# A Flamingo block on one core: attention unit and prologue in a new order, three banks for maximum scores, one for value products, two buffers for raw outputs, near-tile work in halves

## The chip, the cores and the metric

The kernel runs on one core of a Trainium2 chip. The metric is the device time of one execution in microseconds, taken as the median of several runs.

## What is computed

```python
x = x + tanh(g_xattn) * attention(ctx, ctx, layernorm(x), Wk, Wv, Wq, Wo, p_params)
x = x + tanh(g_ffn) * moe(layernorm(x), gate_w, bias, Wg, Wu, Wd, Wg_s, Wu_s, Wd_s)

# attention: B=4, 1024 queries, 154 keys, 16 heads of 16
scores = qh @ kh.T / 4 + rel          # rel: 9 learned values by clip(q - k, -4, 4)
scores = where(q >= k, scores, -1e30)
out = softmax(scores) @ vh @ Wo.T

# moe: 4096 tokens, 8 experts, 4 chosen by grouped top-k of sigmoid scores, and one shared
```

Since there are only 154 keys, the mask and the distance term vary only in the first two tiles of 128 queries of each batch; they are called the near tiles 0 and 1.

## The kernel before

Each engine has its own instruction list, written by hand; semaphores tie the lists together, and nothing reorders them.

**Prologue.** Inputs are loaded; the first half batch (512 queries) is normalised and turned (`transposes`), queries, keys and values are projected. High and low parts are kept (`x_hi`/`x_lo`, `q_out`/`q_lo`, `k_hi`/`k_lo`) so that fast matmuls keep precision. Then the maximum scores of the first half batch are made.

**Units.** The attention is eight units, `unit(b, h, ...)`, two per batch (h=0 and h=1, 512 queries each). The units of batches 1 and 2 are the body of a hardware loop, those of batches 0 and 3 are written out; the text calls the eight u0 to u7. A unit has 20 steps `i`. Each step makes one transposed score tile (`score`, into one of two PSUM banks `sT`), whose exponential ScalarE takes (`ex`); after five steps (a group `g`) the value products follow (`values`, into `oT`), which ScalarE copies to `raw` (`raw_out`). In between the unit does, for other units:

- the maximum scores of the next half batch (`max_scores`, L854, 32 tiles of 128 queries by two heads), each reduced on VectorE (`maximum`, L582). The two k of a pair use the two banks of `smax`, and one stands before the value product and one behind it. For near tiles ScalarE copies the scores out (`near`, L466) to `sx`; GpSimd builds their distance terms (`near`, L380, L392), VectorE adds them, takes the maximum and subtracts it (`tile0` L596 and L599, `tile1` L605 to L616), and GpSimd subtracts for tile 0 (L389);
- the negated maxima (`minus_max`), turned by TensorE (`max_T`, L866), copied to `mt` (`max_out`, L636) and spread by a DMA of SyncE (`m_stack`, L261) into the stack `qs`, for which the first score of the next unit waits;
- normalisation, turning and projection for the unit after the next; SyncE stacks its queries in two parts of six DMAs (`q_stack`, L250) and its keys (`k_stack`);
- the division of the unit before: SyncE takes the sums from `raw` through DRAM (`divisors`, L267 to L277), VectorE takes reciprocals and divides (`divide`, L648), TensorE projects (`project`, L930), VectorE adds the residual (L655).

Projections, turns and copies share two PSUM banks `work` in a fixed order of use (`X_USE` to `Y_USE`); each waits until the use before the last is read (`work_free`).

**Behind the units** the expert part loads its split weights, routes, and finishes the last division, projection and residual (`attend_divide`, `attend_finish`, `attend_residual`); 72 turns of gate, up and down products follow.

## Time and profile before

| | us |
|---|---|
| median of 3 runs | 740.97 (736.86 to 741.93) |
| the profiled execution | 738.62 |
| its span, first to last instruction | 736.7 |
| lead-in, to the first score of u0 | 65.1 |
| attention, u0 to u6 | 275.2 |
| u7 and the start of the expert part | 63.1 |
| the expert turns | 333.3 |
| mean granted TensorE clock | 0.929 of full |

A unit's length is read from the first score of one unit to the first score of the next. "Busy" is how long an engine had an instruction under way; the idle time in brackets at a row names what the instruction waited for last.

### The profile page before, as it was taken

The numbers are of one execution on the slowest core, as the hardware profiler recorded it, in microseconds if no ns is written. First come the engines' busy times: TensorE is split into PE (matmuls) and PEld (weight loads), VectorE is DVE, ScalarE is ACT, GpSimd is POOL, SyncE is SP. The second block draws the span as 40 slices with busy tenths as digits, with TensorE's granted clock in tenths as the row PEclk, the third lists the DMA queues.
The fourth block names the chain that finished last, engine by engine and source line by source line (L and its number), as shares of the span: only waits on it lengthen the run. The fifth ranks groups of instructions, "written<-read, shape, count | busy, mean of one in ns | idle before, by whom it ended". The sixth has DMA issues, their size and how long they took to land.

```text
span 736.7 us, 10646 instructions
## 1 busy us (share of the span) xinstructions
PE 628.5 (85%) x3384; PEld 484.8 (66%) x3384; DVE 460.5 (63%) x884; ACT 277.4 (38%) x501; POOL 176.7 (24%) x177
## 2 busy tenths in 40 slices
PE   3674968788878977888647999999999999999997
PEld 2553745457545754554325888888888888888886
DVE  3567657777578758762168475755747575665653
...
DMA packets 39856, 58.65 MB, mean 80 GB/s; under 512 B 7984, under 2 KB 21040, under 8 KB 39792
## 3 DMA queue, kind: packets, MB, share of 16 engines
...
HBM read 31.76 MB, written 4.85 MB: 50 GB/s over the span
## 4 chain that ended last, share of the span: by engine, by line
issue 49%; PE 20%; DVE 10%; POOL 8%; DMA 6%; SPq 3%; ACT 2%; POOLq 0%; DVEq 0%; ACTq 0%
POOL hl L1150 4%; PE oT L915 4%; PE smax L854 4%; SPq L277 2%; DMA qs<-mt 2%; DVE mx L582 2%; PE oT L919 2%; PE sT L895 2%; DMA at<-rden_d 2%; PE work L794 2%; PE sT L894 2%; DVE mx L609 1%; DMA rden_d<-dent 1%; POOL d L380 1%; PE work L825 1%
## 5 line engine op out<-in xcount | busy, mean ns | idle before, releaser
L1150 POOL TENSOR_TENSOR hl<-sg,hh 128x512 fp32r<-128x512 f32 x72 | 93.0, 1293 | 249.3 <-ACT hh L1193 249.3
L482 ACT ACTIVATE ex<-sT 128x512 f32<-128x512 f32 (+1 forms) x160 | 92.2, 590 | 152.1 <-PE sT L895 127.6
L1187 ACT ACTIVATE sg<-pg 128x512 f32<-128x512 f32 x72 | 43.0, 597 | 198.8 <-PE pu L1432 198.0
L854 PE MATMUL smax<-km,qs 96*128 96x308 f32 (+1 forms) x240 | 91.2, 412 | 27.1 <-DVE mx L582 19.3
L582 DVE TENSOR_REDUCE mx<-smax 128x2 f32<-128x308 f32 x184 | 82.9, 474 | 48.3 <-PE smax L854 45.4
L854 PEld LDWEIGHTS smax<-km,qs 96*128 96x128 f32 x240 | 47.8, 206 | 72.8 <-DVE mx L582 40.1
L1447 PE MATMUL py<-wxl,hh 128*128 128x256 f32 x288 | 81.8, 284 | 3.1 <-DVE x L1331 2.0
L1447 PE MATMUL py<-wxh,hl 128*128 128x256 f32 x288 | 80.9, 281 | 0.0
L1447 PE MATMUL py<-wxh,hh 128*128 128x256 f32 x288 | 80.6, 280 | 0.0
L1319 DVE TENSOR_TENSOR sg<-cwb,sg 128x512 f32<-128x512 f32 x64 | 67.2, 1050 | 11.3 <-DMA cwb<-cwt_d 8.4
L1314 DVE TENSOR_TENSOR sg<-pu,sg 128x512 f32<-128x512 f32 x72 | 49.2, 683 | 28.0 <-ACT sg L1187 26.6
L1432 PE MATMUL pg<-x2l,wxh 128*128 128x512 f32 x144 | 60.6, 421 | 4.1 <-issue 4.1
L895 PE MATMUL sT<-qs,ks 128*128 128x256 f32 (+1 forms) x128 | 52.9, 429 | 12.3 <-DMA qs<-mt 11.0
L1447 PEld LDWEIGHTS py<-wxl,hh 128*128 128x128 f32 x288 | 54.1, 188 | 9.0 <-DVE x L1331 4.3
L1432 PE MATMUL pg<-x2h,wxh 128*128 128x512 f32 x144 | 57.8, 401 | 0.0
L1432 PE MATMUL pu<-x2l,wxh 128*128 128x512 f32 x144 | 57.6, 400 | 0.0
L1432 PE MATMUL pg<-x2h,wxl 128*128 128x512 f32 x144 | 57.5, 400 | 0.0
L1432 PE MATMUL pu<-x2h,wxl 128*128 128x512 f32 x144 | 57.4, 399 | 0.0
L1432 PE MATMUL pu<-x2h,wxh 128*128 128x512 f32 x144 | 56.9, 395 | 0.0
L1447 PEld LDWEIGHTS py<-wxh,hl 128*128 128x128 f32 x288 | 54.1, 188 | 2.7
L1447 PEld LDWEIGHTS py<-wxh,hh 128*128 128x128 f32 x288 | 54.7, 190 | 0.0
L1193 ACT CAST hh<-sg 128x512 fp32r<-128x512 f32 x72 | 44.0, 612 | 9.6 <-DVE sg L1319 9.3
(152 smaller groups left out, 1124.1 us busy)
## 6 DMA issues: line engine op xcount, KB each, us to landing
...
```

The lines of the kernel that those rows point to most:

```text
L482: nc.scalar.activation(ex[:, g % 2, i % 5, q0:HALF], ST[i % 2][:, q0:HALF], ACT.Exp).then_inc(exp_s, 1)
L582: nc.vector.reduce_max(mx[:, m_tile(h, p), 2 * stk:2 * stk + 2], bank[:, k, 0:PAIR].rearrange("p (j k) -> p j k", j=2), AX_X).then_inc(mx_ ...
L854: last_one = nc.tensor.matmul(bank[:, k, 0:width], qs[0:96, s, tile * P:(tile + 1) * P], km[:, s, 0:width], start=True, stop=True)
L895: last_one = nc.tensor.matmul(out[:, q0:HALF], ks[:, s, j * KL:j * KL + P], qs[:, s, q], start=True, stop=True)
L915: nc.tensor.matmul(OT[g % 2][32 * j:32 * j + 32, :], va[:, 4 * g + j, :], ex[:, g % 2, j, :], start=True, stop=True)
L1150: nc.gpsimd.tensor_tensor(hl[:, i % R, :], sg[:, i % R, :], hh[:, i % R, :], ALU.subtract).then_inc(hl_done, 1)
L1187: nc.scalar.activation(sg[:, i % R, :], PG[i % RG][:], ACT.Silu).then_inc(sg_s, 1)
L1193: nc.scalar.copy(hh[:, i % R, :], sg[:, i % R, :]).then_inc(hh_s, 1)
L1314: done = nc.vector.tensor_tensor(sg[:, i % R, :], PU[i % RG][:], sg[:, i % R, :], ALU.mult)
L1319: nc.vector.tensor_tensor(sg[:, i % R, :], cwb[:, e % RC, :], sg[:, i % R, :], ALU.mult)\
L1432: last = nc.tensor.matmul(out_[:], wa[:, e, w], xa[:, u, c, :], start=first, stop=(c == C - 1 and wa is wxh and xa is xh))
L1447: last = nc.tensor.matmul(y, ha[:, i % R, q], wa[:, e, 2 * C * I:XW], start=(e == 0 and s == 0 and j % 2 == 0), stop=(e == NE1 - 1 and s = ...
```

## The change

- PSUM: `smax` has three single banks, used in turn by the tiles q = 2p + k (a ring); `oT` has one bank; in the prologue the ring has five banks (with `sT`).
- `ORDER` gives the maximum scores a new order, in which tile 2 stands between parts of tile 0; they begin at step 0, not 3, and both of a pair stand before the value product.
- In an h=0 unit keys are projected first (steps 1 to 4); turns move to steps 7 and 8, value inputs to 9 and 10, queries to 11 to 14; `minus_max` moves to step 16, `max_T` to 17, the two `project` to 16 and 18, `tile1` to 13 to 15 and 17, `k_hi` and `k_lo` to 16 to 18.
- `raw_first` and `raw` are used by turns, so `raw_out` waits for the division two units back; it moves to steps 4, 9, 14 and 19.
- `divide` goes from VectorE to GpSimd, in an h=1 unit between the distance terms and the subtraction of tile 0.
- Tile 0 and the reduction of tile 1 are done in halves of the heads.
- SyncE: the last `k_stack` and the context load move past `q_stack`; the second half of x is loaded before wv.
- Prologue: `selectors` come first on ScalarE, `k_hi` and `k_lo` go in the three parts of the key projection (`k_hi_first`, `k_lo_first`), the statistics of the second half batch and its normalisation come earlier, its queries are projected in four pieces at p = 6 to 9, and `tile0` at p = 11.
- `minus_max` makes its first part as -2x + x; the input of context has one more, empty batch.

```diff
+    raw_first = sb("raw_first", [P, NG, HALF])
+    raws = (raw_first, raw)
...
-    SM = ctx.enter_context(nc.psum_tensor("smax", [P, 2, HALF], F32))
+    SM = ctx.enter_context(nc.psum_tensor("smax", [P, 3, HALF], F32))
-    M_START = (SM, STP)
-    OT = [ctx.enter_context(nc.psum_tensor(f"oT{i}", [P, HALF], F32)) for i in range(2)]
+    MAX_BANKS = [SM[:, i, :] for i in range(3)]
+    M_START = MAX_BANKS + ST
+    OT = ctx.enter_context(nc.psum_tensor("oT", [P, HALF], F32))
...
-    X_USE, V_USE, Q_USE, K_USE, M_USE, Y_USE = (0, 11), 2, (3, 13), 5, (8, 15), (9, 16)
+    FIRST_USE, K_USE, X_USE, V_USE, Q_USE, Y_USE, M_USE = (0, 11), 0, (3, 11), 5, (6, 13), ((8, 10), (15, 17)), (9, 16)
     K_PARTS = (range(0, 3), range(3, 6), range(6, 8))
 
-    K_STEP, K_READ = (12, 13, 14, 14, 15, 15, 16, 16), (15, 16, 17)
-    M0, NM = 3, TU * NSTK // 2
-
-
-    DIVIDE, TILE0 = ((13, 14), (12, 13)), (10, 11)
+    K_READ = (3, 4, 5)
+    NM = TU * NSTK // 2
+    NEAR = NM
+    ORDER = ((0, 0), (0, 1), (2, 0), (2, 1), (0, 2), (0, 3), (1, 0), (1, 1),
+             (1, 2), (1, 3), (2, 2), (2, 3), (3, 0), (3, 1), (3, 2), (3, 3))
+    RING = 3
+    PER_MAX = 3 * NM
+
+    TILE0, TILE1 = (9, 10, 11, 12), (13, 14, 15)
...
-            if h == 0 and ahead:
-                sp.wait_ge(v_ps, b + 1)
-                sp.nop().then_inc(waited, 1)
-                sp.dma_start(ctxb[:], t["ctx"][b + 1]).then_inc(c_in, 16)
             if carry and (h == 0 or ahead):
                 sp.wait_ge(st_ps, NI * u)
                 q_stack(1 - h, 1)
+            if carry and h == 0:
+                k_stack(NG - 1)
+            if h == 1 and ahead:
+                sp.wait_ge(v_ps, b + 2)
+                sp.nop().then_inc(waited, 1)
+                sp.dma_start(ctxb[:], t["ctx"][b + 2]).then_inc(c_in, 16)
             if carry:
-                divisors(u - 1)
+                divisors(u - 1, 1 - h)
...
                 m_stack(b + 1, 0)
-                sp.wait_ge(st_ps, NI * (u + 1))
-                k_stack(NG - 1)
...
+        def divide(u, h):
+            pool.wait_ge(rden_in, 128 * (u + 1))
+            pool.wait_ge(shift_in, 64 * (u + 1))
+            pool.nop().then_inc(waited, 1)
+            for g in range(2):
+                nc.gpsimd.tensor_tensor(at[:, g, :], raws[h][:, g, :], at[:, g, :], ALU.mult).then_inc(at_s, 1)
...
+                for half in (slice(0, H // 2), slice(H // 2, H)) if i == 0 else (slice(0, H),):
...
+            if between is not None:
+                divide(between, 0)
+            for i, half in enumerate((slice(0, NSTK // 2), slice(NSTK // 2, NSTK))):
+                pool.wait_ge(sadd_s, 7 * b + 3 + i)
+                nc.gpsimd.tensor_tensor(keys[:, half], keys[:, half], largest[:, half], ALU.subtract).then_inc(sub0_s, 1)
...
+            if carry and not (h == 1 and ahead):
+                divide(u - 1, 1 - h)
             if h == 1 and ahead:
-                near(b + 1, False)
+                near(b + 1, False, u - 1)
                 pool.wait_ge(st_ps, NI * (u + 1))
...
-        def raw_out(u, g, start=False):
+        def raw_out(u, h, g):
             act.wait_ge(pv_ps, NG * u + g + 1)
-            if not start:
-                act.wait_ge(at_s, 2 * (u - 1) + g % 2 + 1)
-            nc.scalar.copy(raw[:, g, :], OT[g % 2][:]).then_inc(raw_s, 1)
+            if not (isinstance(u, int) and u < 2):
+                act.wait_ge(at_s, 2 * (u - 1))
+            nc.scalar.copy(raws[h][:, g, :], OT[:]).then_inc(raw_s, 1)
...
-                if i == 5 and carry:
-                    raw_out(u - 1, 3, start=(h == 1 and isinstance(b, int) and b == 0))
-                if i == 6 and ahead:
-                    x_hi(u + 2, NW0 + X_USE[h])
-                if i == 11 and ahead:
+                if i == 4 and carry:
+                    raw_out(u - 1, 1 - h, 3)
+                if i in (8, 9) and ahead:
+                    x_hi(u + 2, NW0 + X_USE[h], (i - 8,))
+                if i == 13 and ahead:
                     for part in range(2):
                         act.wait_ge(qs_in[1 - h][part], 16 * 6 * (b + h + 1))
-                if i in (11, 13) and ahead:
-                    q_out(u + 2, NW0 + Q_USE[h], ((i - 11) // 2,))
+                if i in (13, 15) and ahead:
+                    q_out(u + 2, NW0 + Q_USE[h], ((i - 13) // 2,))
                 if ahead and h == 1:
-                    if i == M0:
+                    if i == 0:
                         act.wait_ge(sub_s, 3 * (b + 1))
-                    if i >= M0 and i - M0 < NM and m_tile(0, i - M0) < 2:
-                        near(b + 1, i - M0)
-                if i in (14, 17, 19):
-                    raw_out(u, (14, 17, 19).index(i), start=not carry)
-                if ahead and h == 0 and i == 19:
-                    k_hi(b + 1, False)
-
+                    if i < NM and m_tile(0, i) < 2:
+                        near(b + 1, i)
+                if i in (9, 14, 19):
+                    raw_out(u, h, i // 5 - 1)
+                if ahead and h == 0 and i in (16, 17):
+                    k_hi(b + 1, (i - 16,))
...
+                if i < NM and (h == 0 or ahead and m_tile(mh, i) >= 2):
+                    maximum(mb, mh, i)
+                if i in (0, 1) and ahead:
+                    tile_stats(b + 1, h, (2 * i, 2 * i + 1))
+                if i == 2 and ahead:
                     norm_stats(b + 1, h)
-                if i in (3, 4) and ahead:
-                    normalised(b + 1, h, (2 * (i - 3), 2 * (i - 3) + 1))
-                if i == 6 and ahead:
-                    x_lo(u + 2, NW0 + X_USE[h])
+                if i in (5, 6) and ahead:
+                    normalised(b + 1, h, (2 * (i - 5), 2 * (i - 5) + 1))
                 if i in K_READ and ahead and h == 0:
                     part = K_READ.index(i)
                     k_in(b + 1, NW0 + K_USE + part, part)
-                if i == 10 and ahead and h == 0:
+                if i in (9, 10) and ahead:
+                    x_lo(u + 2, NW0 + X_USE[h], (i - 9,))
+                if i == 8 and carry:
+                    reciprocals(u - 1)
+                if i == 11 and ahead and h == 0:
                     v_in(b + 1, NW0 + V_USE, False)
-                if i == 9 and carry:
-                    reciprocals(u - 1)
-                if i in DIVIDE[h] and carry:
-                    divide(u - 1, (DIVIDE[h].index(i),))
                 if diagonal and i in TILE0:
                     tile0(b + 1, TILE0.index(i))
-                if i in (11, 13) and ahead:
-                    q_lo(u + 2, NW0 + Q_USE[h], ((i - 11) // 2,))
+                if i in (14, 16) and ahead:
+                    q_lo(u + 2, NW0 + Q_USE[h], ((i - 14) // 2,))
+                if diagonal and i in TILE1:
+                    tile1(b + 1, TILE1.index(i))
...
-                if i == 18:
+                if i == 16 and (h == 0 or ahead):
+                    minus_max(mb, mh)
+                if i in (16, 18):
+                    pr = (i - 16) // 2
+                    if carry:
+                        residual(b - 1 + h, 1 - h, pr, NW0 + Y_USE[h][pr])
+                    else:
+                        unused(1, b, Y_USE[h][pr])
+                if i == 17:
                     if h == 0 or ahead:
-                        minus_max(mb, mh)
-                        if diagonal:
-                            tile1(b + 1, 0)
                         max_out(mb, mh, NW0 + M_USE[h])
                     else:
                         unused(1, b, M_USE[h])
-                if i == 19:
                     if diagonal:
-                        tile1(b + 1, 1)
-                        tile1(b + 1, 2)
-                    if h == 0 and ahead:
-                        k_lo(b + 1)
-                    if carry:
-                        for pr in range(2):
-                            residual(b - 1 + h, 1 - h, pr, NW0 + Y_USE[h] + pr)
-                    else:
-                        unused(2, b, Y_USE[h])
+                        tile1(b + 1, 3)
+                if h == 0 and ahead and i in (17, 18):
+                    k_lo(b + 1, (i - 17,))
...
+        dve.wait_ge(x_in[0], 16)
+        tile_stats(0, 1)
+        norm_stats(0, 1)
         q_lo(0, 2)
-        dve.wait_ge(x_in[0], 16)
-        norm_stats(0, 1)
+        k_in(0, 4, 0)
+        k_in(0, 5, 1)
+        k_lo_first(0)
         normalised(0, 1)
-        for part in range(3):
-            k_in(0, 4 + part, part)
+        k_in(0, 6, 2)
         v_in(0, 7, True)
-        k_lo(0)
+        k_lo_first(1)
+        k_lo_first(2)
         x_lo(1, 8)
         for p in range(NM):
-            if p == NM // 2:
-                q_lo(1, 10)
             if m_tile(0, p) >= 2:
-                maximum(0, 0, p, M_START[p % 2])
-            if p == 8:
-                for part in range(2):
+                maximum(0, 0, p, M_START)
+            if p in (7, 9):
+                q_lo(1, 10, ((p - 7) // 2,))
+            if p == 11:
+                for part in range(4):
                     tile0(0, part)
         minus_max(0, 0, start=True)
...
+            q = 2 * p + k
+            if q == 0:
+                pe.wait_ge(mx_s, PER_MAX * b + NM * h)
+            elif q >= RING and is_near(h, q - RING):
+                pe.wait_ge(sx_s, NEAR * b + copied(q - RING + 1))
+            elif q >= RING:
+                pe.wait_ge(mx_s, PER_MAX * b + NM * h + reduced(h, q - RING + 1))
+            stack_scores(m_tile(h, p), p, k, MAX_BANKS[q % RING])
...
-                if not (start and g < 2):
-                    pe.wait_ge(raw_s, NG * u + g - 1)
+                if not (start and g == 0):
+                    pe.wait_ge(raw_s, NG * u + g)
                 for j in range(4):
-                    nc.tensor.matmul(OT[g % 2][32 * j:32 * j + 32, :], va[:, 4 * g + j, :], ex[:, g % 2, j, :],
+                    nc.tensor.matmul(OT[32 * j:32 * j + 32, :], va[:, 4 * g + j, :], ex[:, g % 2, j, :],
...
-                if seeks:
-                    max_scores(b + h, 1 - h, i - M0, 0)
+                if i < NM and (h == 0 or ahead):
+                    for k in range(2):
+                        max_scores(b + h, 1 - h, i, k)
                 if i in (1, 3) and carry:
                     values(b - 1 + h, 1 - h, NG - 1, i // 2)
                 if i > 5 and i % 5 in (1, 3):
                     values(b, h, i // 5 - 1, i % 5 // 2, start)
-                if seeks:
-                    max_scores(b + h, 1 - h, i - M0, 1)
-                if i in (5, 6) and ahead:
-                    transposes(u + 2, b, X_USE[h], (i - 5,))
-                if i in (7, 8) and ahead and h == 0:
-                    values_in(b + 1, b, V_USE, ((0, 1), (2, 3, 4))[i - 7])
-                if i in (9, 10, 11, 12) and ahead:
-                    queries(b, X_USE[h], Q_USE[h], (i - 9,))
-                if ahead and h == 0:
-                    keys(b + 1, b, K_USE, [s for s in range(NSTK) if K_STEP[s] == i])
-                if i == 19:
-                    if h == 0 or ahead:
-                        max_T(b + h, 1 - h, b, M_USE[h])
-                    if carry:
-                        for pr in range(2):
-                            project(b - 1 + h, 1 - h, pr, b, Y_USE[h] + pr)
+                if ahead and h == 0 and i in (1, 2, 3, 4):
+                    keys(b + 1, b, K_USE, (2 * i - 2, 2 * i - 1))
+                if i in (7, 8) and ahead:
+                    transposes(u + 2, b, X_USE[h], (i - 7,))
+                if i in (9, 10) and ahead and h == 0:
+                    values_in(b + 1, b, V_USE, ((0, 1), (2, 3, 4))[i - 9])
+                if i in (11, 12, 13, 14) and ahead:
+                    queries(b, X_USE[h], Q_USE[h], (i - 11,))
+                if i == 17 and (h == 0 or ahead):
+                    max_T(b + h, 1 - h, b, M_USE[h])
+                if i in (16, 18) and carry:
+                    pr = (i - 16) // 2
+                    project(b - 1 + h, 1 - h, pr, b, Y_USE[h][pr])
```

Rows of the change have its own line numbers.

TensorE at the end of the last h=0 unit, u6, before (`nm` are the negated maxima, `at` the divided outputs):

```order
L919 MATMUL oT<-ex,vb 128x384 [waits exp]
L854 MATMUL smax<-km,qs 128x308 [waits mx]
L899 MATMUL sT<-idr,tp 128x128 [waits exp]
L901 MATMUL sT<-qs,k 128x256 x2
L866 MATMUL work<-idr,nm 32x128 [waits nm,work_free]
L866 MATMUL work<-idr,nm 32x128 x3
L930 MATMUL work<-wo,at 128x256 [waits work_free,at]
L930 MATMUL work<-wo,at 128x256 x3
L930 MATMUL work<-wo,at 128x256 [waits work_free,at]
L930 MATMUL work<-wo,at 128x256 x3
L895 MATMUL sT<-qs,ks 128x512 [waits ms_in,exp]
```

The same place in the change:

```order
L998 MATMUL work<-wo,at 128x256 [waits work_free,at]
L998 MATMUL work<-wo,at 128x256 x3
L962 MATMUL sT<-idr,sx 128x128 [waits exp]
L962 MATMUL sT<-idr,sx 128x128
L963 MATMUL sT<-qs,ks 128x256
L933 MATMUL work<-idr,nm 32x128 [waits nm,work_free]
L933 MATMUL work<-idr,nm 32x128 x3
L962 MATMUL sT<-idr,sx 128x128 [waits exp]
L962 MATMUL sT<-idr,sx 128x128
L963 MATMUL sT<-qs,ks 128x256
L987 MATMUL oT<-ex,vb 128x384 [waits exp]
L998 MATMUL work<-wo,at 128x256 [waits work_free,at]
L998 MATMUL work<-wo,at 128x256 x3
```

The turn of the maxima (L866, now L933) has left its place behind the last score, and the two projections stand apart from each other and before scores that are still to come.

VectorE in the h=1 unit of the loop, before, from the work on tile 0:

```order
L599 TENSOR_REDUCE mx<-sx 128x16
L551 TENSOR_TENSOR ql<-work,qh 128x512
L645 REGISTER_ALU
L646 REGISTER_ALU
L648 TENSOR_TENSOR at<-raw,at 128x512 x2
L551 TENSOR_TENSOR ql<-work,qh 128x512
L581 REGISTER_ALU
L582 TENSOR_REDUCE mx<-smax 128x2
L581 REGISTER_ALU
L582 TENSOR_REDUCE mx<-smax 128x2
```

The same list in the change, around the second low part of the queries:

```order
L606 TENSOR_TENSOR ql<-work,qh 128x512
L681 REGISTER_ALU
L682 TENSOR_REDUCE mx<-sx 128x8
L648 REGISTER_ALU
L649 TENSOR_REDUCE mx<-smax 128x2
L648 REGISTER_ALU
L649 TENSOR_REDUCE mx<-smax 128x2
L682 TENSOR_REDUCE mx<-sx 128x8
L606 TENSOR_TENSOR ql<-work,qh 128x512
L696 ISA
L699 SCALAR_TENSOR_TENSOR nm<-mx 128x2x16
L702 SCALAR_TENSOR_TENSOR nm<-mx,nm 128x2x16
```

The second `ql`, which frees SyncE's first part of `q_stack`, stood ahead of eight reductions of `smax`; now it stands behind all of them and behind both halves of tile 1's maximum, and the division is gone.

GpSimd in the h=1 unit of the loop, before, with tile 0 subtracted (L389) ahead of tile 1's terms:

```order
L380 TENSOR_TENSOR d<-relr,cst 128x2048
L386 REGISTER_ALU
L389 TENSOR_TENSOR sx<-sx,mx 128x8x2x128
L362 REGISTER_ALU
L366 REGISTER_ALU
L369 COPY relc<-sx 128x64
```

The same list in the change, from tile 1's terms on:

```order
L417 TENSOR_TENSOR d<-relr,cst 128x512
L422 REGISTER_ALU
L423 TENSOR_TENSOR d<-d,cst 128x512
L370 ISA
L371 REGISTER_ALU
L374 TENSOR_TENSOR at<-raw_first,at 128x512 x2
L430 REGISTER_ALU
L431 TENSOR_TENSOR sx<-sx,mx 128x4x2x128
L430 REGISTER_ALU
L431 TENSOR_TENSOR sx<-sx,mx 128x4x2x128
```

The subtraction of tile 0 is now two instructions at the end, behind the division.

## Rows read from the trace of the kernel before

**Rows 1.** Windows: length, busy PE, PEld, DVE, ACT, POOL, granted clock, DMA share, GB/s.
```profile
0.00:65.10 65.10, 33.50 (x134) 26.17 (x135) 35.99 (x76) 18.72 (x37) 19.42 (x28) 0.75 0.59 165
...
103.20:145.10 41.90, 34.14 (x142) 19.84 (x142) 26.75 (x41) 20.57 (x44) 15.21 (x16) 0.87 0.38 89
145.10:185.50 40.40, 34.94 (x224) 25.49 (x224) 31.31 (x66) 17.56 (x30) 2.25 (x4) 1.00 0.34 78
185.50:225.10 39.60, 31.76 (x143) 18.85 (x143) 27.68 (x45) 20.46 (x44) 15.21 (x16) 0.91 0.39 95
225.10:306.00 80.90, 68.81 (x367) 45.76 (x367) 59.66 (x110) 38.13 (x74) 17.56 (x20) 0.94 0.36 85
306.00:340.30 34.30, 28.68 (x152) 19.38 (x153) 21.09 (x43) 13.13 (x24) 0.98 (x2) 0.90 0.57 167
340.30:403.40 63.10, 39.77 (x154) 23.62 (x155) 27.71 (x66) 25.31 (x42) 3.49 (x5) 0.81 0.17 45
403.40:736.70 333.30, 326.09 (x1872) 281.99 (x1872) 202.58 (x381) 106.19 (x177) 101.33 (x84) 0.99 0.19 61
```

**Rows 2.** Timeline of PE in u2 and u3.
```profile
179.53 0.61 PE L866 MATMUL work<-idr,nm 128*32 128x128 f32 x4 [0.96 <-DVE nm L627]
...
179.98 3.62 PE L930 MATMUL work<-wo,at 128*128 128x256 f32 x16
...
185.50 0.73 PE L895 MATMUL sT<-qs,ks 128*128 128x512 f32 x2 [1.91 <-DMA qs<-mt]
...
212.31 0.62 PE L854 MATMUL smax<-km,qs 96*128 96x308 f32 x1 [3.89 <-DVE mx L582]
...
225.09 0.43 PE L894 MATMUL sT<-idr,sx 128*128 128x128 f32 x2 [1.99 <-DVE tp L616]
```

**Rows 3.** Chain that ended last, in order of time, at the end of u2.
```profile
180.99 4.47 DMA qs<-mt
```

**Rows 4.** Timeline of SyncE's queue in u2 and u3.
```profile
170.83 1.31 SPq L250 DMA_DIRECT2D qs<-qh  x2
...
173.47 1.24 SPq L250 DMA_DIRECT2D qs<-qh  x2
...
180.99 0.59 SPq L261 DMA_DIRECT2D qs<-mt  x1
...
220.27 0.58 SPq L261 DMA_DIRECT2D qs<-mt  x1
```

**Rows 5.** Timeline of DVE in u3.
```profile
207.64 3.62 DVE L648 TENSOR_TENSOR at<-raw,at 128x512 f32<-128x512 f32 x2 [0.66 <-DMA at<-rden_d]
...
211.19 0.68 DVE L551 TENSOR_TENSOR ql<-work,qh 128x512 fp32r<-128x512 f32 x1
...
211.79 0.85 DVE L582 TENSOR_REDUCE mx<-smax 128x2 f32<-128x308 f32 x2
...
220.48 2.72 DVE L609 TENSOR_REDUCE mx<-sx 128x16 f32<-128x2464 f32 x1 [0.23 <-DVE mt L636]
```

**Rows 6.** GpSimd: timeline in u3.
```profile
206.47 3.61 POOL L389 TENSOR_TENSOR sx<-sx,mx 128x2048 f32<-128x2048 f32 x1 [4.72 <-DVE mx L599]
```

**Rows 7.** The page's costliest groups, GpSimd's first.
```profile
L1150 POOL TENSOR_TENSOR hl<-sg,hh 128x512 fp32r<-128x512 f32 x72 | 93.0, 1293 | 249.3 <-ACT hh L1193 249.3
```

**Rows 8.** Timeline of the prologue: PE.
```profile
34.19 0.39 PE L854 MATMUL smax<-km,qs 96*128 96x316 f32 x1 [1.92 <-DVE km L575]
...
65.11 0.66 PE L894 MATMUL sT<-idr,sx 128*128 128x128 f32 x2 [8.55 <-DVE tp L616]
```

**Rows 9.** Timeline of the prologue: GpSimd, then DVE.
```profile
41.04 3.65 POOL L380 TENSOR_TENSOR d<-relr,cst 128x2048 f32<-128x2048 f32 x1
...
59.68 0.66 DVE L605 TENSOR_TENSOR sx<-sx,d 128x480 f32<-128x480 f32 x1 [2.67 <-POOL d L392]
```

**Rows 10.** Timeline of SyncE in u6, of ScalarE in u7.
```profile
324.51 4.61 SPq L1107 DMA_DIRECT2D wx<-in_wx  x9
...
358.67 0.59 ACT L472 COPY raw<-oT 128x512 f32<-128x512 f32 x1 [5.86 <-DVE at L648]
```

260 lines of the change are left out of this document (138 added, 122 removed).

## The prediction

> **What bounds the kernel now.** I first cut the span at the first score of each unit [rows 1]. The expert turns take 333.3 us with TensorE busy for 326.1 of them; no line of them changes, so they stay. What the change can touch is the lead-in of 65.1 us, the units u0 to u6, and the 63.1 us of u7 with the start of the expert part. In the loop a batch costs 80.0 us (u2 40.4, u3 39.6) and the next 80.9. There TensorE is busy for 34.9 and 31.8 us and VectorE for 31.3 and 27.7: neither is full, the two wait for each other.
>
> Next the waits of TensorE in u2 and u3 [rows 2]. At the end of u2 it waits 0.96 us for the negated maxima, turns them, projects for 3.62 us and then waits 1.91 us for the spread of the maxima, whose DMA takes 4.47 us from issue to landing [rows 3]. In u3 it waits 3.89 us for a reduction and at the end 1.99 us for the subtractions of tile 1. The 3.89 us come from VectorE's queue [rows 5]: two divisions that stand there as 3.62 us together, during which GpSimd subtracts tile 0 for 3.61 us [rows 6]. Last the lead-in: the first maximum score starts at 34.2 us, and the first score waits 8.55 us [rows 8], because tile 1's terms come from GpSimd late, after a term of 3.65 us for tile 0 and the subtraction behind it [rows 9].
>
> **The lead-in.** The selectors fill a time in which ScalarE waits, the second half's statistics one in which VectorE waits, and the low parts of the keys are made in three parts while TensorE still projects. Walking VectorE's list with the old durations, the last low part is ready near 28.5 instead of 34.2: 5.7 us. Tile 0's scores are copied some 6 us earlier, so the two halves of its term (3.65 us together [rows 9]) end near 38.5, and tile 1's terms near 43, before VectorE asks. VectorE then is the chain: the last queries' low part near 39 to 40.5, two pairs of maxima, tile 0 in four parts of 1.15, four pairs at 0.85 [rows 5], `minus_max`, turn and copy 1.6, and then for tile 1 the add of 0.66 [rows 9], the reduction of 2.72 [rows 5] and 1.8 of subtractions. That gives 55 to 57.5; I take 56.1, a gain of 9.0. The 2.67 us wait for GpSimd [rows 9] is gone; what is late next is VectorE itself. Bounds: 7 (queries at half clock as before) and 11.5 (full clock).
>
> **An h=0 unit (u2, u4).** TensorE's instructions stay: of its 34.9 busy us [rows 1] some 31.4 are left when the rows at half clock are counted at full. The unit now ends by a different chain: second low part of the queries (step 16), six DMAs of `q_stack`, the DMA of the maxima, landing. SyncE's queue is what is new here. Before, the six were issued from 170.83 to 174.71, long before the maxima's at 180.99 [rows 4]; now they start only at step 16, and the maxima's stand behind them. TensorE's list up to step 15 is 15 scores (5.2), 15 pairs of maximum scores (4.4), three sets of value products (4.2), keys (4.4), turns (0.9), value inputs (1.8), queries (2.8): 23.7 us. I add 2 us for the half clock after the wait at the start, 2.5 us where turns and value inputs wait for VectorE (it must do pairs of maxima, keys and the normalisation first), 0.6 for changes between kinds of matmul: 28.8. Score, exponential, copy and low part bring 31.0; plus 3.9 for the six issues [rows 4], plus 4.5 for the DMA [rows 3], 39.4 against 40.4. The wait for maxima of 0.96 is gone, but the wait for the DMA grows from 1.91 to about 3, since only 3.6 us of work stand behind the turn. Bounds: 37.4 without the half clock and the changes, 41 if the DMA is held up by the six before it.
>
> **An h=1 unit (u3, u5).** The division leaves VectorE: 3.62 us of its queue [rows 5]. Pairs of maxima no longer stop TensorE for 3.89 us, since the ring lets it run three tiles ahead. But the start is paced by ScalarE, which copies 16 near tiles between its exponentials and frees the ring: its list ends step 8 near 13.5 us. From there VectorE has, up to the second low part, both `x_lo`, six pairs of maxima (6 x 0.8), tile 0 in four parts (4.6), tile 1's add and maximum (0.84 + 2.72), two low parts: 15.7 us with no gap. GpSimd works at the same time: half a term, tile 1's terms, the division, both subtractions. The price of that is in the trace: two divisions that with nothing on GpSimd take 1.3 us took 3.62, and the first began 1.2 us after GpSimd's 3.61 [rows 5, 6]. So a two-input instruction waits nearly to the end of GpSimd's. Three of VectorE's meet one now (two tile 0 adds, tile 1's add); I take 2.6 us for them, between 0 and 4. That puts the second low part at 13.5 + 15.7 + 2.6 = 31.8, where it stood at 211.87 - 185.50 = 26.4 before [rows 2, 5]. Then 3.9 us of issues [rows 4] and about 3.7 for the smaller DMA of the maxima: 39.3, against 39.6 and, for u5, 40.4. In u3 what ended last was tile 1 (1.99 us); now the subtractions of tile 1 (3 us) hide behind the DMA, and the DMA is last. Bounds: 36.5 with no meeting, 41 with all.
>
> The loop's two batches so come to 78.7 each: 80.0 - 78.7 = 1.3 and 80.9 - 78.7 = 2.2, together 3.5.
>
> The Trainium skill, SBUF — State Buffer, "Who interferes with whom", says that a VectorE instruction with two SBUF inputs contends with a GpSimd instruction that reads SBUF, the loser blocking fully, and that `tensor_reduce` never does. The 3.62 us beside 3.61 us [rows 5, 6] agree with the first; the second is why halves of the maxima would go unharmed. The rule speaks against putting the division on GpSimd in an h=1 unit.
>
> **The others.** u0 and u1 take 80.0 us together, from 65.1 to 145.1 [rows 1]. u0 has no old division and gets the same chain at its end: 0.5 gained. u1 was 41.9 [rows 1] because of a half clock after a long wait; as an h=1 unit it comes to 39.4: 2.5. Together 3.0.
>
> u6 has no projections for later batches and no near tiles. Its 34.3 us hold a wait for the division. Now the division goes: old outputs copied one step earlier, sums and reciprocals through DRAM as before (at 18 instead of 19 us), 2 x 1.29 on GpSimd [rows 7] = 20.6; projection, score and turn 23.2, copy 24; the DMA would land at 28.5. But the nine weight loads are issued from 324.51 to 329.1 [rows 10], 1 us earlier now, and their data fill the queues until about 29; the maxima's DMA stands behind them: 30.3. Gain 4.0, between 2 and 6.
>
> u7: ScalarE's wait of 5.86 for the division [rows 10] goes with the second buffer. TensorE instead waits at step 16 for the same division, which ends at 20 us of the unit (17.1 + 2.6), but only scores of three steps are left behind it where before six were: about 1.0 gained. In the start of the expert part the two divisions leave VectorE between routing and weights: 1.1. Together 2.1; bounds 0 and 4.
>
> One value bank, the raw buffers' extra SBUF, the six additional VectorE and GpSimd halves outside those counted: nothing, as the copy of `oT` stands two steps ahead of the next group's products.
>
> **The sum.** 9.0 + 3.0 + 3.5 + 4.0 + 2.1 = 21.6. The profiled execution took 738.6 (span 736.7 and 1.9 around it), so 717.0. It lies 2.4 us under the median of the three runs; I leave it there.
>
> **The rivals.**
>
> *VectorE is not held up.* If the meetings cost nothing and half clock is rare, an h=1 unit is 36.5 (3 x 2.8 more) and an h=0 unit 37.4 (2 x 2 more), the lead-in 2 us better: 14 more, 703. For it speaks that most of VectorE's new work are reductions and reads of PSUM, against it the 3.62 us.
>
> *The maxima's DMA is held up by the six before it.* Each unit's end then has 1.5 us more (a queue with 768 KB ahead of it), seven times 1.5 is 10.5, 727. For it: 512 KB alone took 4.47 us [rows 3] with nothing ahead.
>
> *Slower: GpSimd becomes the pace of the h=1 units.* The subtraction of tile 0, which the next unit's first score needs, now stands behind the division, and that behind a chain through DRAM. Rows of u3 have the divisors landed 22.1 us into the unit (207.64 - 185.50 [rows 2, 5]). Division and first half of the subtraction need 2.6 + 1.8, so it decides from a landing at 35 us on; to eat 21.6 us, three units would need 7.2 us each, a landing at 42. Nothing in the trace points there. 742.
>
> *It doesn't do what it says.* The ring could stay unused if the reader of the tile before is late anyway; then the units keep 80 us a batch and the lead-in and u6, u7 remain: 738.6 - 15.1 = 723.5, inside the second rival's case.
>
> **How the numbers follow.** 0.57 for my walk (710 to 722), 0.20 for VectorE unhindered (698 to 709), 0.18 for the held-up DMA or unused ring (722 to 731), 0.05 for the slower one. The range 701 to 729 leaves out a little on both sides. A change under 1% (7.4 us, about what can be told from none here) needs a time above 731: 0.04; slower by more, 0.03; faster 0.93.
>
> **What the new profile would show.** First score at 55 to 58; the first maximum score near 28.5. In the loop each unit 38 to 41 us, with TensorE's largest wait at the first score, 2 to 4 us, put down to the DMA `qs<-mt`; that DMA issued directly behind a `q_stack`. No wait of ScalarE for `at`, no wait of TensorE of over 2 us for `mx` in an h=1 unit. VectorE's halves of the tile 0 add over their 1.15 us. I am wrong if the h=1 units stay near 40 and wait for `sub0` or `at` (GpSimd), or fall under 37 (no meetings), or if the lead-in gains less than 6.

## The result, and the profile after

The changed kernel takes 734.39 us (median of 15 runs, 731.84 to 737.08) against 741.93 us for the kernel before (15 runs, 736.86 to 744.55): ratio 0.9904, 95% interval 0.9884 to 0.9923. It is 1.0% faster, where 717 us (3.4% less than 741.93) was forecast, and it lies outside the range of 701 to 729.

The windows of the changed kernel, cut at each unit's first score as in [rows 1] (us; busy PE, PEld, DVE, ACT, POOL; granted clock, DMA share, GB/s):

```profile
58.70:97.30 38.60, 29.86 (x199) 23.17 (x199) 27.05 (x62) 16.83 (x29) 1.22 (x2) 0.94 0.18 42
97.30:136.80 39.50, 31.34 (x142) 19.61 (x142) 25.20 (x44) 20.51 (x44) 18.77 (x20) 0.93 0.39 95
136.80:178.20 41.40, 35.26 (x225) 26.01 (x225) 28.23 (x64) 17.54 (x30) 4.72 (x6) 0.96 0.33 77
178.20:215.90 37.70, 30.31 (x143) 19.42 (x143) 25.38 (x44) 20.46 (x44) 18.90 (x20) 0.95 0.39 95
215.90:256.40 40.50, 35.10 (x225) 26.23 (x225) 27.96 (x64) 17.54 (x30) 4.72 (x6) 0.96 0.36 81
256.40:294.10 37.70, 30.35 (x142) 19.23 (x143) 25.67 (x45) 20.46 (x44) 18.93 (x20) 0.95 0.39 95
294.10:329.50 35.40, 27.78 (x153) 19.16 (x153) 16.18 (x38) 13.13 (x24) 3.48 (x4) 0.89 0.59 172
329.50:397.60 68.10, 43.77 (x155) 26.32 (x155) 26.10 (x62) 25.09 (x42) 8.96 (x9) 0.75 0.16 42
397.60:731.80 334.20, 327.08 (x1872) 282.71 (x1872) 202.37 (x381) 106.13 (x177) 101.05 (x84) 0.99 0.19 60
```

Against [rows 1]: the lead-in went from 65.1 to 58.7 us, u1 from 41.9 to 39.5, the h=1 units to 37.7 each. But u2 grew from 40.4 to 41.4, u6 from 34.3 to 35.4, and u7 with the start of the expert part from 63.1 to 68.1 us. VectorE's busy time in u2 fell from 31.3 to 28.2 us and the unit still got longer: less work on VectorE alone did not make it shorter.

Where TensorE waits in the loop is seen in its timeline (start, busy, idle before and what ended it), at the end of u2 and of u3:

```profile
178.16 0.79 PE L963 MATMUL sT<-qs,ks 128*128 128x512 f32 x1 [3.94 <-DMA qs<-mt]
...
208.85 0.39 PE L933 MATMUL work<-idr,nm 128*32 128x128 f32 x2 [1.56 <-DVE nm L702]
...
215.89 0.69 PE L962 MATMUL sT<-idr,sx 128*128 128x128 f32 x2 [3.36 <-DMA qs<-mt]
```

and SyncE's queue shows what stood ahead of that DMA:

```profile
168.87 1.32 SPq L273 DMA_DIRECT2D qs<-qh  x2
170.23 1.25 SPq L273 DMA_DIRECT2D qs<-ql  x2
171.52 1.24 SPq L273 DMA_DIRECT2D qs<-qh  x2
172.88 1.34 SPq L284 DMA_DIRECT2D qs<-mt  x1
...
208.58 1.27 SPq L273 DMA_DIRECT2D qs<-qh  x2
209.90 1.24 SPq L273 DMA_DIRECT2D qs<-ql  x2
211.18 1.24 SPq L273 DMA_DIRECT2D qs<-qh  x2
212.56 0.58 SPq L284 DMA_DIRECT2D qs<-mt  x1
```

`mt` was whole at 171.97 and at 209.91 (VectorE's copies start at 171.29 and 209.51); in u3 the DMA so left 2.65 us late. Before, the six copies were out by 174.7 and the maxima's DMA left at 180.99, as soon as it could [rows 4]. TensorE's waits for it went from 11.0 us in 4 places to 25.5 us in 6; a seventh, 3.28 us ahead of u6's first score, is listed without a releaser but ended as that DMA landed.

The waits for the maxima's banks did go. In the listing by line, the row of the maximum scores gives their busy time, the mean of one product in ns and TensorE's idle time ahead of them, before and after:

```profile
L854 PE MATMUL smax<-km,qs 96*128 96x308 f32 (+1 forms) x240 | 91.2, 412 | 27.1 <-DVE mx L582 19.3 <-ACT sx L466 4.7 <-DVE km L575 1.9
```

```profile
L921 PE MATMUL smax<-km,qs 96*128 96x308 f32 (+1 forms) x244 | 71.2, 348 | 10.6 <-ACT sx L516 4.5 <-DVE mx L649 2.9 <-DVE km L631 1.7
```

A further 4.9 us of waiting for `mx` stand in the prologue, where the ring also uses the banks of `sT`.

The end of the attention part, in SyncE's, GpSimd's and TensorE's timelines:

```profile
314.20 4.57 SPq L1169 DMA_DIRECT2D wx<-in_wx  x9
322.39 0.67 SPq L284 DMA_DIRECT2D qs<-mt  x1
336.67 0.55 SPq L292 DMA_DIRECT2D den_d<-raw_first  x1
...
345.03 3.57 SPq L302 DMA_DIRECT2D at<-rden_d  x8
```

```profile
350.61 2.48 POOL L374 TENSOR_TENSOR at<-raw_first,at 128x512 f32<-128x512 f32 x2 [33.45 <-DMA at<-rden_d]
```

```profile
317.21 3.05 PE L998 MATMUL work<-wo,at 128*128 128x256 f32 x8 [2.84 <-POOL at L374]
...
329.48 1.19 PE L963 MATMUL sT<-qs,ks 128*128 128x512 f32 x2 [4.77 <-DMA qs<-mt]
...
353.14 3.35 PE L998 MATMUL work<-wo,at 128*128 128x256 f32 x7 [6.67 <-POOL at L374]
...
362.73 1.06 PE L983 MATMUL oT<-ex,va 128*32 128x512 f32 x8 [1.25 <-ACT raw L523]
```

The first of these waits is u6's, for the same kind of division. In u7 TensorE reaches step 16 at 346.5 and stands for 6.67 us before the projection; the scores of steps 17 to 19, the last value products and everything of the expert part are queued behind it.

### The profile page after: what moved, and what is told of

Its sections match the earlier page's. It is cut to its first block, busy times and chain, and to the rows that moved or that the text cites. A ratio compares the mean times of both kernels' runs of the same rounds, so it can differ in the third digit from the quotient of the medians.

```text
span 731.8 us, 10675 instructions
## 1 busy us (share of the span) xinstructions
PE 618.5 (85%) x3384; PEld 484.1 (66%) x3384; DVE 441.6 (60%) x884; ACT 277.4 (38%) x505; POOL 202.4 (28%) x201
## 4 chain that ended last, share of the span: by engine, by line
issue 46%; PE 22%; DVE 11%; DMA 7%; POOL 6%; SPq 5%; ACT 2%; POOLq 0%; DVEq 0%; ACTq 0%
POOL hl L1212 4%; DMA qs<-mt 4%; PE smax L921 3%; DVE mx L649 3%; PE oT L983 3%; SPq L273 2%; PE work L897 2%; PE work L866 2%; PE sT L963 2%; PE oT L987 2%; PE sT L962 2%; PE work L998 1%; DVE sx L667 1%; SPq L302 1%; DVE mx L682 1%
## 5 line engine op out<-in xcount | busy, mean ns | idle before, releaser
L649 DVE TENSOR_REDUCE mx<-smax 128x2 f32<-128x308 f32 x187 | 79.4, 470 | 60.7 <-PE smax L921 60.1
L921 PE MATMUL smax<-km,qs 96*128 96x308 f32 (+1 forms) x244 | 71.2, 348 | 10.6 <-ACT sx L516 4.5
L963 PE MATMUL sT<-qs,ks 128*128 128x256 f32 (+1 forms) x128 | 55.7, 443 | 19.4 <-DMA qs<-mt 18.1
L963 PEld LDWEIGHTS sT<-qs,ks 128*128 128x128 f32 x128 | 26.5, 210 | 31.9 <-issue 16.6
```

The costliest lines, as they stand in the source:

```text
L649: nc.vector.reduce_max(mx[:, m_tile(h, p), 2 * stk:2 * stk + 2], banks[q % len(banks)][:, 0:PAIR].rearrange("p (j k) -> p j k", j=2), AX_X)\
L921: last_one = nc.tensor.matmul(bank[:, 0:width], qs[0:96, s, tile * P:(tile + 1) * P], km[:, s, 0:width], start=True, stop=True)
L963: last_one = nc.tensor.matmul(out[:, q0:HALF], ks[:, s, j * KL:j * KL + P], qs[:, s, q], start=True, stop=True)
```

## The experiments

Each run's ratio is to runs of the kernel before on the same chip; "unit" lengths are from one unit's first exponential to the next one's, by ScalarE's timeline (changed kernel: 39.4, 41.5, 37.8, 40.2, 38.0 for u1 to u5). A gain in us is a difference of medians from 734.39 us. The runs were on several chips, on which the kernel before took 738.6 to 742.8 us, so gains of 1 or 2 us say nothing by themselves.

**The copies from `qh` ahead of those from `ql`** (the edit in words).

```diff
-  wait work_free (ql whole); wait st_ps; q_stack(h, 0)            # qh, ql, qh
+  wait st_ps; wait q_hi; q_stack(h, 0, (0, 2))                     # four from qh
+  wait work_free (ql whole); q_stack(h, 0, (1,))                   # two from ql
```

> In the loop units SyncE issues the four q_stack copies whose source is qh as soon as qh is whole, and only the two from ql afterwards, so two issues instead of six (0.65 us each) stand between ql and the maxima's DMA. The theory of the queue: TensorE's largest wait at a unit's first score (3.94 us at 178.16, 3.36 us at 215.89) is for qs<-mt, and that DMA stood behind the six. With mt ready at 171.97 and 209.91 its issue moves from 172.88 to about 172.0 in an h=0 unit and from 212.56 to about 210.1 in an h=1 unit; each of the five units 1 to 5 that carry it gets 0.9 us (h=0) or 2.4 us (h=1) shorter, about 8 us in all, 726 us (range 722 to 730). The rival, that other work is right behind (the subtractions of tile 1 end at 213.0, the half clock lasts as long after any wait): at most 0.5 us a unit, 731 to 735 us, with the wait's releaser now sx or tp.

Measured: 715.17 us (714.01 to 718.74), ratio 0.9663, interval 0.9597 to 0.9728: 19 us faster than the changed kernel, more than twice what I expected. The queue's part came as expected. SyncE's and TensorE's timelines at the end of u2 and u3:

```profile
164.53 1.23 SPq L274 DMA_DIRECT2D qs<-ql  x2
165.87 0.59 SPq L285 DMA_DIRECT2D qs<-mt  x1
...
199.57 1.24 SPq L274 DMA_DIRECT2D qs<-ql  x2
201.01 0.58 SPq L285 DMA_DIRECT2D qs<-mt  x1
```

```profile
170.41 0.49 PE L966 MATMUL sT<-qs,ks 128*128 128x512 f32 x1 [2.34 <-DMA qs<-mt]
...
204.19 0.43 PE L965 MATMUL sT<-idr,sx 128*128 128x128 f32 x2 [0.60 <-DVE sx L690]
```

The waits shrank by 1.6 and 2.8 us, and at the end of u3 the wait is now for VectorE's subtraction. But u1 to u5 take 34.7, 38.3, 33.8, 38.3 and 35.2 us, 1.9 to 4.7 less each. A part of the rest is the clock. Windows of 6 us from a unit's first score, of the changed kernel (start of u3 and u4), then of this one (the same two):

```profile
178.20:184.20 6.00, 5.95 (x27) 4.13 (x27) 1.21 (x7) 3.78 (x8) 0.00 (x0) 0.73 0.50 116
...
215.90:221.90 6.00, 6.00 (x35) 4.58 (x36) 3.37 (x10) 1.77 (x3) 0.00 (x0) 0.74 0.57 134
```

```profile
170.40:176.40 6.00, 5.94 (x32) 3.89 (x33) 3.08 (x12) 3.76 (x9) 1.05 (x2) 1.00 0.55 129
...
204.20:210.20 6.00, 6.00 (x44) 4.83 (x45) 4.63 (x15) 2.37 (x6) 0.68 (x4) 1.00 0.74 171
```

TensorE is full in all four; at a mean grant of 0.73 it is at 1.2 GHz for about half of the 6 us and loses 1.6 us. In the kernel before, u3's window after its wait of 1.91 us had 1.00. The length of the wait alone doesn't decide here: after 2.34 us at 170.4 the grant was 1.00, after 2.26 us at 242.5 in the same run 0.72.

**The same edit in the kernel before.**

> The kernel before the change with the same edit: qh copies first. There the maxima came at step 19 and mt was ready only at 180.6, some 6 us after the last copy (ql issued at 173), so no copies stood ahead of the maxima's DMA. If the queue is a cost that came with the change (max_T two steps earlier, queries two steps later), this run takes what the kernel before takes, 740 to 742 us. If the earlier qh copies help by themselves (the copies for the next unit's maximum scores land sooner), it is faster by 3 us or more.

Measured: 740.54 us, ratio 1.0007, interval 0.9981 to 1.0033. So the early copies bring nothing by themselves. The queue is a cost that came with the change's new order.

**The wait filled with matrix products.**

```diff
+  if i == 19 and (h == 0 or ahead):
+      for _ in range(17 if h == 0 else 14):
+          matmul(MAX_BANKS[2], idr, cmask in 512 columns, start=True, stop=True)
```

> The changed kernel, with 17 (h=0) or 14 (h=1) matrix products of 512 columns into an unused bank of the maxima put behind step 19, where TensorE stands for the maxima's DMA for 3.3 to 4.1 us; their results are not used, and nothing else moves. The theory of the clock: in the changed kernel the granted clock of the first 6 us after each such wait was 0.72 to 0.74, in the run with the qh copies first, whose waits were 2.3 and 0.6 us, 1.00, and each fall costs about 1.6 us (0.27 of 6 us); with the wait filled the clock stays at 1.00 and the six units that begin behind such a wait get 1.2 to 1.6 us shorter each, though the DMA lands no sooner: 724 to 728 us. The rival, that the stretch behind the wait is paced by ScalarE's and VectorE's work whatever TensorE's clock: 733 to 736, with the filling itself making it slower where it outlasts the wait.

Measured: 725.13 us (721.13 to 729.46), ratio 0.9763, interval 0.9694 to 0.9831: 9.3 us faster than the changed kernel, with work added and the DMA's place in the queue as it was. TensorE's timeline at the end of u2, then the window of the first 6 us of u3:

```profile
170.06 4.05 PE L1026 MATMUL smax<-cmask,idr 128*128 128x512 f32 x17
173.95 0.39 PE L963 MATMUL sT<-qs,ks 128*128 128x512 f32 x1
```

```profile
174.00:180.00 6.00, 5.95 (x34) 3.91 (x33) 1.90 (x8) 3.91 (x9) 1.21 (x2) 1.00 0.42 98
```

The grant at the start of u3 is 1.00 where the changed kernel had 0.73, and it is 1.00 in the first 6 us of u2 to u6, where it was 0.72 to 0.74. At u1 it rose from 0.53 to 0.72. At u7 it stayed low (0.61, before 0.54): there the DMA took 9.9 us to land behind the weight loads, and TensorE waited another 4.29 us behind the filling. In the two profiled executions u1 to u5 are 1.9, 1.6, 0.9, 0.7 and 1.3 us shorter from first score to first score, 6.4 in sum, and u6 is no shorter. So the theory of the clock holds and its rival does not, at 0.7 to 1.9 us for a unit and not at an even 1.5. The lowest and highest of the four runs are 8 us apart, so 9.3 is no sharper than a few us. By subtraction, about 10 of the 19.2 us would be left for the DMA that leaves and lands sooner; no run measures that part alone.

**Weight loads behind the maxima's DMA in u6.** `load_weights()` moved from ahead of `m_stack(b, 1)` to behind it.

> In unit 6 the nine weight loads are issued behind the maxima's DMA instead of ahead of it. If the weights' traffic is what made that DMA land 7.1 us after its issue (5.2 us in unit 2, same size), TensorE's wait of 4.77 us at the first score of unit 7 shrinks to about 3 us and the reading and writing of the divisors for unit 6 in unit 7 is as fast or slower, since the loads then run beside it: 731 to 734 us in all. If the issue order does not matter, no change, 734. If the loads now collide with the divisors (den_d, dent, rden_d, at, from 336 to 350 us) or come too late for the casts of the weights, slower: 736 to 739.

Measured: 732.76 us (731.58 to 734.55), 1.6 us less, but inside the spread of the changed kernel's runs; what the trace shows is surer than the gain. TensorE's and SyncE's timelines:

```profile
327.05 0.69 PE L964 MATMUL sT<-qs,ks 128*128 128x512 f32 x2 [2.19 <-DMA qs<-mt]
...
351.85 3.78 PE L999 MATMUL work<-wo,at 128*128 128x256 f32 x8 [10.32 <-POOL at L375]
```

```profile
331.73 0.56 SPq L292 DMA_DIRECT2D den_d<-raw_first  x1
338.96 0.33 SPq L294 DMA_DIRECT2D dent<-den_d  x1
```

Two expectations hold at once. The maxima's DMA landed 4.4 us after its issue instead of 7.0, the wait for it fell from 4.77 to 2.19 us, and u7 began at a grant of 1.00 instead of 0.54. But the divisors' write now runs beside the loads, 7.2 us instead of 2.2 to the next issue, so that TensorE, sooner at step 16, waits 10.32 us for the division instead of 6.67.

**Projections and residuals late.** All of them at step 19, behind `max_T` (its bank used at 8 and 15, theirs at 9, 10, 16, 17).

> Both projections and both residuals stand at step 19 again in every unit, behind max_T, as before the change; all else as changed. If the early place of the projections costs time where the divided outputs come late, the 6.67 us for which TensorE waits for GpSimd at 353.14 and the 2.84 us of unit 6 go beside the scores of steps 17 to 19, and unit 7 with the start of the expert part gets 4 to 6 us shorter, unit 6 about 1 to 2 us: 726 to 730 us. If the loop units lose by it (sixteen matmuls, 3.6 us, at the unit's end instead of under the maxima's chain), each gets up to 1 us longer, and the sum is 730 to 735. If the divided outputs are what the rest waits for anyway, no change: 734.

Measured: 725.54 us (723.77 to 726.18), ratio 0.9791, interval 0.9731 to 0.9851, 8.9 us faster. The units got shorter too (39.2 and 36.8 us for u2 and u3, from 41.5 and 37.8), which I hadn't expected. The projections now fill a time in which TensorE waited: the wait ahead of u2's first score fell from 4.10 to 0.54 us and the one ahead of u4's from 3.36 to 0.14, and u2, u3, u4 and u6 began at a grant of 1.00 where it had been 0.72 to 0.74. That is the clock again, in a second run.

**Only u6's projections moved**, behind u7's last value products on TensorE, and behind the first normalisation of the expert part on VectorE.

```diff
-  if i in (16, 18) and carry: project(b - 1 + h, 1 - h, ...)
+  if i in (16, 18) and carry and (h == 0 or ahead): project(b - 1 + h, 1 - h, ...)
   ...
   values(B - 1, 1, NG - 1, short)
+  for pr in range(2): project(B - 1, 0, pr, B - 1, 16 + pr)
```

> The changed kernel, with the projections and residuals of unit 6 alone moved, out of unit 7 to behind its last value products (TensorE) and behind the first normalisation of the expert part (VectorE). If the 5.0 us by which unit 7 and the start of the expert part got longer are TensorE standing for GpSimd's divided outputs at step 16 (6.67 us) with the last scores, values and everything of the expert part queued behind it, the last score moves from about 361 to about 350 us, the divided outputs (353.1) come while VectorE normalises, and the expert part begins 10 to 13 us earlier: 722 to 725 us. If only a copy of the wait comes back behind the value products, as in the run with the projections late everywhere, 728 to 731.

Measured: 723.38 us (722.5 to 725.06), ratio 0.9767, interval 0.972 to 0.9814: 11.0 us faster by this one edit. TensorE's timeline:

```profile
351.45 1.06 PE L985 MATMUL oT<-ex,va 128*32 128x512 f32 x8 [1.25 <-ACT raw L523]
...
354.94 3.72 PE L1000 MATMUL work<-wo,at 128*128 128x256 f32 x16 [1.37 <-POOL at L374]
360.27 0.63 PE L1462 MATMUL pm<-cst,xn 128*128 128x128 f32 x4 [1.62 <-DVE xn L1308]
```

The last value products start at 351.5 instead of 362.7, the expert part's transposes at 360.27 instead of 370.92, and the division's end is met with 1.37 us of waiting.

**Two banks instead of three.** `RING = 2`, in the units alone.

> Inside the units the maximum scores use 2 banks instead of 3, all else as changed. If the third bank is what shortened the waits for mx (27.1 us in sum before, 10.6 us after), they come back and the seven units get 0.5 to 1.5 us longer each: 738 to 745 us. If the gain came from the new order of the steps alone, no change within 2 us: 732 to 736.

Measured: 741.37 us (738.23 to 747.07), ratio 1.0004, interval 0.9972 to 1.0036: 7.0 us slower than the changed kernel. Units u0 to u6 are each 0.8 to 2.2 us longer, so the time came as the first theory had it. Its mechanism did not. The same row, with two banks:

```profile
L921 PE MATMUL smax<-km,qs 96*128 96x308 f32 (+1 forms) x244 | 76.1, 370 | 10.7 <-ACT sx L516 5.2 <-DVE mx L649 2.3 <-DMA qs<-qh 2.0
```

The idle time ahead of these products stayed at 10.7 us (10.6 with three banks, 27.1 before), and the waits for `mx` in it were 2.3 us (2.9 and 19.3). So it is the rest of the change (the new order of the steps, the division off VectorE), not the third bank, that took those waits away. The third bank is worth about as much as the whole change brought, but how is not shown: the products themselves are longer (370 ns against 348), u2 and u4 begin at a grant of 0.50 instead of 0.72 and 0.74, and in u6 the maxima's DMA took 9.5 us behind the weight loads instead of 7.0. That last one need not come from the bank: in the other runs that leave the loads ahead of that DMA it took 6.7 to 10.0 us.

**The prologue: normalisation of the second half later.** The transposes of the second half, their copies and the normalisation behind the first two pairs of maximum scores.

> The changed kernel with the transposes of the second half of batch 0, their copies on ScalarE and the normalisation on VectorE moved behind the first two pairs of maximum scores. The theory that VectorE's queue ahead of km set the first maximum score (30.95 us against the 28.5 forecast; the normalisation of 1.38 us stands at 26.11, between the two thirds of km): the first maximum score comes at about 29.5, the first score at 57.2 to 58 instead of 58.66, 733 us. The rival, that VectorE has the same work to do either way up to the first score (it is named in nearly all of the chain from 26 to 58.6): first maximum score earlier, first score unmoved within 0.5 us, 734 to 735.

Measured: 734.00 us (732.43 to 734.51). TensorE's timeline:

```profile
29.50 0.60 PE L922 MATMUL smax<-km,qs 96*128 96x316 f32 x1 [5.20 <-DMA qs<-qh]
...
59.67 0.66 PE L963 MATMUL sT<-idr,sx 128*128 128x128 f32 x2 [6.09 <-DVE tp L691]
```

The first maximum score came 1.45 us sooner, now waiting for the queries' DMA, and the first score 1.0 us later, twice what the rival allowed but the same in its sense: an earlier first maximum score did not bring an earlier first score. In neither order did the first maximum score come at 28.5.

**Three together**: copies from `qh` first, weights late, projections late.

> The qh copies first, both projections at step 19, and the weight loads behind the maxima's DMA, together. If the three causes are separate, their gains over the changed kernel (19.2, 8.9 and 1.6 us) add up: 704.7 us, range 701 to 708. If two of them removed the same wait (the projections ahead of max_T hold up mt on VectorE, and the copies hold up the DMA behind it), the sum is less: 708 to 713.

Measured: 713.73 us (710.1 to 716.62), against 715.17 for the first alone: no better beyond the spread. With the copies first, u3 takes 36.6 us here against 33.8: with no projection at step 16 to fill it, TensorE waits for the negated maxima at step 17, and the waits for `nm` went from 7.2 us in 5 places to 13.2 in 7. In its timeline, near the end of u3, the wait grew from 1.55 to 3.30 us, and the two products behind it run at half clock (1.02 us in the run with the copies alone):

```profile
201.66 0.61 PE L937 MATMUL work<-idr,nm 128*32 128x128 f32 x2 [3.30 <-DVE nm L706]
201.92 0.78 PE L967 MATMUL sT<-qs,ks 128*128 128x512 f32 x1
202.50 1.91 PE L991 MATMUL oT<-ex,vb 128*128 128x512 f32 x2
```

**All of that, and the maxima's DMA in two** (stacks 0 and 1, then 2 to 7).

> As all_three, with the maxima's DMA in two: stacks 0 and 1, which steps 0 to 4 read, first, and stacks 2 to 7 behind, awaited at step 5. In the h=0 units of the run with the qh copies first, this DMA still took 4.5 us from its issue at 165.87 to TensorE's score at 170.41 with TensorE idle for 2.34 us. If its size sets that time (512 KB; the half as large one of an h=1 unit took 3.3 us), the quarter lands about 1.5 to 2 us sooner and the four units that end in an h=0 one get that shorter: 4 to 8 us below all_three. If a fixed part of 2 to 3 us sets it, 0 to 3 us below; if the second issue (0.6 us) delays the q_stack copies that the maximum scores of step 4 need, no gain.

Measured: 706.7 us (705.98 to 708.41), ratio 0.9549, interval 0.9524 to 0.9575: 7.0 us less. TensorE's waits for the maxima's DMA fell from 9.5 us in 3 places to 4.7 in 2: at the end of u0 from 5.40 to 3.26, of u2 from 2.04 to 1.47 only, of u4 from 2.10 to nothing. The two profiled executions differ by only 1.7 us, so which of the 7 us are waits and which clock they can't tell.

**The best of it.** Copies first, DMA in two, u6's projections behind the last products, the loop's left where the change put them:

> The qh copies first, the maxima's DMA in two, and the projections of unit 6 behind the last value products; projections in the loop at steps 16 and 18 as changed, weight loads ahead of the maxima's DMA as changed. From split_mask (706.7 us): the loop's h=1 units, where the late projections left TensorE waiting for nm, go from 36.2 and 37.0 us back to 33.8 (as with the qh copies alone), 5 to 8 us; at the end TensorE no longer waits 7.5 us ahead of the last value products, 6 to 10 us. 690 to 697 us. If the queue and the late projections had each hidden the other's limit (the sum of single gains over all_three was wrong by 9 us), 698 to 703.

Measured: 700.92 us (699.96 to 704.8), 4 us above my range of 690 to 697, and inside the 698 to 703 of the case that two limits hide each other. Two places stand out. u5 is back at 35.4 us, but u3 takes 36.9: its first score waits only 0.36 us and yet its first 6 us are granted 0.72, of which 1.36 us go to a wait for `km`. And the maxima's DMA, again behind the weight loads, keeps u7's first score for 4.91 us:

```profile
306.95 1.19 PE L974 MATMUL sT<-qs,ks 128*128 128x512 f32 x2 [4.91 <-DMA qs<-mt]
```

The same, and the nine weight loads behind u6's divisors:

> As best_a, with the weights' nine loads behind the reading and writing of unit 6's divisors, so that neither the maxima's DMA (7.1 us beside the loads, against 5.2) nor that of the divisors (den_d took 2.2 us alone, 6.4 us beside the loads in split_mask) runs beside them. If those two stand on the path at the end, 3 to 6 us below best_a. If the loads then come too late for ScalarE's casts, whose first is needed some 15 us after the last score, up to 5 us above.

Measured: 695.77 us (692.88 to 696.82), ratio 0.9385, interval 0.9336 to 0.9434: 5.2 us less than without. u6 takes 28.0 us instead of 32.7, and u7's first score waits 0.19 us. The loads now run beside the divisors of u7 itself, whose write took 7.2 us to the next issue. This version beats both kernels, by 6.2% and 5.3%.

## Why the prediction was wrong

The profiled execution with the prediction's sum would have a span of 715.1 us (717.0 less the 1.9 around it); it has 731.8. Step by step, forecast, measured (from first score to first score) and the difference:

```
lead-in        56.1   58.7   +2.6
u0             37.6   38.6   +1.0
u1             39.4   39.5   +0.1
u2, u4         39.4   41.4, 40.5   +3.1
u3, u5         39.3   37.7, 37.7   -3.2
u6             30.3   35.4   +5.1
u7 + start     61.0   68.1   +7.1
expert turns  333.3  334.2   +0.9
```

**u7: the step that failed most.** "TensorE instead waits at step 16 for the same division ... but only scores of three steps are left behind it ...: about 1.0 gained." What I took for the harmless side was the harmful one. Behind the stalled projection stood not three scores but the last value products, the last sums and the start of the expert part, in order; moving u6's two projections gave 11.0 us. So u7 with the start of the expert part lost 5.0 us where I had 2.1 gained. The division was also later, done 23.6 us into the unit (at 353.1) and not at 20. Part of that is u7's start, whose first 6 us were granted 0.54: in the run with the loads late, where they were granted 1.00, the divisors' write was issued 4.7 us into the unit instead of 7.2.

**u6: mechanism right, its size missed.** A gain of 4.0 us was forecast and 1.1 us were lost. The maxima's DMA did stand behind the weight loads, landing 7.0 us after its issue. But the copy of the maxima was forecast at 24 us into the unit and the DMA was issued at 28.3. The unit began at a grant of 0.72, and the projection ahead of the maxima waited 2.84 us for GpSimd and then ran at half clock. These had no term in the walk. The loads cost what two pairs of runs show: u6 is 2.9 us shorter with the loads late alone, and 4.7 us shorter in the last run than in the one before it. And I did not see that the divisors are written on the same queues: wherever the loads are put, they meet something, in the last run the divisors of u7. The Trainium skill, DMA: Bandwidth & Descriptors, "Queues, rings and completion order", says that what one sequencer issues is taken by each DMA engine in the order of issue; the 7.2 us of the divisors' write behind nine loads, against 2.2 us with no loads ahead, agree with it.

**h=0 units: the chain was right, its terms 1 to 2 us too small.** The chain, second low part, six issues, maxima's DMA, is the one in the new trace. In u2 the low part came at 31.8 us into the unit (31.0), the maxima's issue at 36.1 (34.9) and the score 5.3 behind it (4.5), which makes the 2.0 us. The named bound of 41 was for a DMA held up by the six before it. u2 went beyond it with a landing only 0.8 us later, and in u4, with the same six ahead, the DMA landed in 4.53 us, as long as the 4.47 with nothing ahead. What the six cost is the time to issue them, and the walk had it.

**The echo.** The chain ends in a wait of TensorE of 3.2 to 4.8 us, and a part at half clock follows it. u2 to u7 all begin with a granted clock of 0.54 to 0.74, where before u2, u3, u5, u6 and u7 began at 1.00 and only u4 at 0.72. (It varies between executions: in the run of the kernel before with the early copies u3 began at 0.72 too.) For h=0 units I had 2 us for it, about what they lost; for u3, u5, u6 and u7 nothing, where 0.72 to 0.74 over 6 us is 1.6 to 1.7 us and u7's 0.54 is 2.8. Filling the wait gave 9.3 us, the better order of the copies 19.2.

**h=1 units: better than forecast**, though they too began at half clock, since VectorE was held up less. I took 2.6 us for meetings with GpSimd; the first half of tile 0's add took 2.63 us where the second took 1.21, and tile 1's 1.01 where it took 0.66 in the prologue, so 1.8 us were left, and the second low part was ready 30.3 us into the unit (31.8). The rule that I quoted from the Trainium skill (SBUF — State Buffer, "Who interferes with whom") agrees with that half beside GpSimd's term. It is no argument against the division there: from 199.98 to 202.53 us it found VectorE mostly at reductions. The wait for `mx` is gone, as forecast, but not for the reason given: with two banks it did not come back, so it was the rest of the change and not the third bank. (The sum of this walk is 39.4, not 39.3.)

**The lead-in: the right last link, a first one too early.** VectorE is the chain up to the first score, as said, and the wait for GpSimd's terms is gone. The keys' low part ended at 30.8, not 28.5, as the second half's normalisation and the values' copies stand between its parts; the run that moved them gained nothing, as VectorE's list is as long either way.

**u0, u1.** The size of u1 held, by luck: it began at a grant of 0.53, which the walk had taken away, and made it up where the h=1 units were better than forecast. u0 got 0.5 us longer, not shorter, by a DMA wait of 6.13 us at its end.

**The rivals.** The time fell beyond the second rival's 727, and not for its mechanism: of its 1.5 us at each landing, 0.8 came in u2 and 0.1 in u4. None of the four rivals held the wait at u7's projection or the echo in every unit. Unhindered VectorE nearly happened in the h=1 units (37.7 against 36.5), without its 703. GpSimd as the pace of the h=1 units did not come, but in u6 and u7 it was what TensorE waited for. The signs that I had named for the loop came true to within 1 us; I had named none for u6 and u7, where 12.2 of the 16.7 us were lost.
